# A mixture-of-experts loop in 36 tiles instead of 39: four tiles shared by two experts, split across column groups of the matmul array

## The chip, the cores and the metric

One core of a Trainium2 chip runs the whole program. The time is device microseconds of one execution, the median over several. TensorE (PE) multiplies, VectorE (DVE) and ScalarE (ACT) work element by element, GpSimd (POOL) does small arithmetic and issues the indirect DMAs, SyncE (SP) issues the plain ones. A matmul has a stationary operand (loaded first, PEld in the profile) and a moving one that streams through the array, and writes PSUM; everything else here is in SBUF or DRAM. An fp32 matmul shows as two matmul rows and two weight loads in the trace.

## The reference, cut to what matters

Eight sublayers on x of 8 x 256 tokens of 256 values. The change touches the sixth, a mixture of 8 experts, two per token:

```python
N, C = 2048, 640                         # B*T tokens, int(1.25 * N / E * K)
top_v, top_i = top_k(softmax(x_flat @ router_w.T), 2)
top_v = top_v / sum(top_v)
for k in range(2):
    eid, gate = top_i[:, k], top_v[:, k]
    pos = (place of the token among those that chose eid as their k-th) 
    keep = pos < C                        # else the token is dropped for this k
    h = gelu(einsum('ech,ehf->ecf', expert_in, w1))     # 256 -> 1024
    y = einsum('ecf,efh->ech', h, w2)                   # 1024 -> 256
    out = out + y[slot] * (gate * keep)[:, None]
x = x + tanh(g_ffn[2]) * out
```

## The kernel before

The 4096 pairs of a token and an expert are sorted by expert and cut into tiles of 128 rows, each of one expert. With 8 experts 4096 / 128 + 7 = 39 tiles (`MT`) are enough for any split, and 39 are always computed; unused rows point at spare rows. Both weight matrices of all experts lie in the SBUF tile `experts`.

**Routing** ends in one long chain on DVE (`Chain.link` is an instruction and a wait for it, `Chain.step` an instruction alone). It makes each expert's first tile (`til`, `end`, `off`) from the counts `cnt`, each pair's place (`cumo`, `where`), one-hot matrices that PE multiplies to invert the order (`spots`, `onehot`, L2578), and from them `rown` (the row to gather for each place), `eid` (the expert of each tile), `gidx` (where its gate lies) and `dest` (the row to add to). PE runs matmuls without use (`warm`) meanwhile.

**The loop** runs over tiles j. POOL gathers the 128 rows of tile j from DRAM (L731, into `xsb`, three buffers), three tiles behind it the gates (L737), and six behind it adds a finished tile to `token_sum` in DRAM by an indirect DMA with addition (L747, from `ysb`, three buffers); a scatter waits until the one before has landed, since two tiles may hold one token. DVE copies the expert's first matrix into `tilew` in two halves (`tile_weights`, L1833, each with a register load of the expert's number, L1831, ahead of it) and the turned rows into `xTb` (L1867). On PE, in the order of the program:

- `rows_t(j+1)`, L2593: two transposes of a gathered tile;
- `first(j)`, L2605: rows to the 1024 hidden values, `tilew` stationary, the 128 rows moving, so that the hidden values come out turned; 16 matmuls of 128 columns, the second half first (semaphores `m_hh`, then `m_h`);
- `second(j-1)`, L2616: eight matmuls of 256 columns, `hidT` stationary, the second expert matrix moving straight out of `experts` at an address in a register.

ACT applies gelu to the two PSUM banks of `first` (L1198) and scales the result by the gate into `ysb` (L1207). So each of these has the time of another tile's matmuls to finish.

**SP** loads the weights of the next layer (`w3a`, `w3b`, `w3f`, `bc3`, `b2`, L494 to L496) ahead of the loop, then the second half of the start values of `token_sum` (L476), and the gates (L501).

Of the kernel before, what the change touches and what calls it, by code (L numbers as in the profile page):

```python
# [13 lines left out]
B, S, D = 8, 256, 256  # L14
# [16 lines left out]
MT = B * S * 2 // P + E - 1  # L31
# [8 lines left out]
def build(nc, a, out, phases=8):  # L40
# [10 lines left out]
    with ctx:  # L51
# [143 lines left out]
        cols = sb("cols", [P, 20])  # L195
# [45 lines left out]
        dest = sb("dest", [P, MT], i32)  # L241
        gate2 = sb("gate2", [P, TT, 2])
        eid = sb("eid", [P, MT], i32)
# [9 lines left out]
        ye = post[3].rearrange("p (t d) -> p t d", t=TB)  # L253
        onehot = [w[:, 0:2, :].rearrange("p c s -> p (c s)").bitcast(bf16).rearrange("p (v n) -> p v n", n=P) for w in wk]
# [20 lines left out]
        STORES = KEPT + 2 * 16  # L275

# [79 lines left out]
        m_ys = counted("m_ys")  # L356
        s_bw2 = sem("s_bw2")
# [30 lines left out]
        GATED = 40  # L388
# [40 lines left out]
        def _(sp):  # L429
# [27 lines left out]
            if phases >= 6:  # L457
# [40 lines left out]
                sp.wait_ge(m_xp.sem, m_xp.past(2))  # L498
                base_rows(B // 2, B)
                sp.wait_ge(rt_v.sem, rt_v.past(GATED))  # L500
                sp.dma_start(gate_d.rearrange("(p n) o -> p (n o)", p=P), gsent).then_inc(s_kd, 16)  # L501
                for u in range(3):
                    sp.wait_ge(s_st[u], MT // 3 * 16)
# [14 lines left out]
        def _(gp):  # L518
# [205 lines left out]
            if phases >= 6:  # L724
# [3 lines left out]
                for j in range(MT + 6):  # L728
                    if j < MT:
                        gp.wait_ge(m_xp.sem, m_xp.past(max(j - 2, 0)))  # L730
                        gp.indirect_dma_start(xsb[j % 3], None, xs_d,  # L731
                                              bass.IndirectOffsetOnAxis(ap=rown[:, j:j + 1], axis=0)
                                              ).then_inc(s_ld[j % 3], 16)
                    if j == 3:
                        gp.wait_ge(s_kd, STORES)
                    if 0 <= j - 3 < MT:
                        gp.indirect_dma_start(gslot[:, j - 3:j - 2], None, gate_d,  # L737
                                              bass.IndirectOffsetOnAxis(ap=gidx[:, j - 3:j - 2], axis=0)
                                              ).then_inc(s_ld[j % 3], 16)
                    if j == 6:  # L740
                        gp.wait_ge(inv_d, 1)
                    if j >= 6:
                        i, u = j - 6, (j - 6) % 3
                        gp.wait_ge(m_ys.sem, m_ys.past(i + 1))
                        if i:
                            gp.wait_ge(s_st[(i - 1) % 3], 16 * ((i - 1) // 3 + 1))
                        gp.indirect_dma_start(acc_d, bass.IndirectOffsetOnAxis(ap=dest[:, i:i + 1], axis=0),  # L747
                                              ysb[u], None, compute_op=ALU.add).then_inc(s_st[u], 16)
# [31 lines left out]
        def _(ac):  # L780
# [401 lines left out]
            if phases >= 6:  # L1182
# [18 lines left out]
                def result(j):  # L1201

                    ac.wait_ge(m_y.sem, m_y.past(j + 1))
                    if j >= 3:
                        ac.wait_ge(s_st[j % 3], 16 * (j // 3))
                    ac.wait_ge(s_ld[j % 3], landed(j + 3))
                    nc.scalar.activation(ysb[j % 3], bank(4)[:, 0:D], ACT.Copy, scale=gslot[:, j:j + 1]  # L1207
# [109 lines left out]
        def _(ve):  # L1317
# [237 lines left out]
            if phases >= 4:  # L1555
# [108 lines left out]
                def l5_zeros():  # L1664
                    nc.vector.memset(sum0[:, lead - 16:lead], 0.0).then_inc(rt_n.sem, 1)
                    nc.vector.memset(small[:, 0:36], 0.0).then_inc(rt_n.sem, 1)
# [80 lines left out]
            if phases >= 5:  # L1747
# [7 lines left out]
                for b in range(B - 4, B - 1):  # L1755
# [6 lines left out]
                til, til2, til3, end = small[:, 0:12], small[:, 12:24], small[:, 24:36], small[:, 36:44]  # L1762
                off, raw = small[:, 48:64], small[:, 64:80]
# [3 lines left out]
                c5.link(nc.vector.tensor_tensor(raw[:, 0:8], cnt[:, 0:8], cnt[:, 8:16], ALU.add))  # L1767
                c5.link(nc.vector.tensor_scalar(raw[:, 8:16], raw[:, 0:8], 1.0 / P, (P - 1) / (2.0 * P),
                                                ALU.mult, ALU.add))
                c5.link(nc.vector.tensor_scalar(raw[:, 0:8], raw[:, 8:16], MAGIC, None, ALU.add))  # L1770
                c5.link(nc.vector.tensor_scalar(til[:, 4:12], raw[:, 0:8], MAGIC, None, ALU.subtract))
                c5.link(nc.vector.tensor_tensor(til2[:, 4:12], til[:, 4:12], til[:, 3:11], ALU.add))
                c5.link(nc.vector.tensor_tensor(til3[:, 4:12], til2[:, 4:12], til2[:, 2:10], ALU.add))
                c5.link(nc.vector.tensor_tensor(end, til3[:, 4:12], til3[:, 0:8], ALU.add))
                c5.link(nc.vector.tensor_tensor(raw[:, 0:8], end, til[:, 4:12], ALU.subtract))
                c5.link(nc.vector.tensor_scalar(off[:, 0:8], raw[:, 0:8], float(P), -1.0, ALU.mult, ALU.add))
# [6 lines left out]
                                                off.unsqueeze(1).broadcast_to([P, TT, 16]), ALU.add))  # L1783
                c5.link(nc.vector.tensor_tensor(hit, cumo, oh, ALU.mult))
# [22 lines left out]
                for k in range(3):  # L1807
# [11 lines left out]
                past = ptall[:, 5 * MT:5 * MT + 7 * MT].rearrange("p (n e) -> p n e", e=E - 1)  # L1819
                ef = here.rearrange("p q j -> p (q j)").bitcast(f32)[:, 0:MT]  # L1820
                c5.link(nc.vector.tensor_tensor(past, iota[:, 0:MT].unsqueeze(2).broadcast_to([P, MT, E - 1]),
                                                end[:, 0:E - 1].unsqueeze(1).broadcast_to([P, MT, E - 1]), ALU.is_ge))
# [988 lines left out]
```

## Time and profile before

| | |
|---|---|
| median of 3 runs | 961.45 us (958.54 to 962.52) |
| the profiled execution | 959.38 us, of which the span from first to last instruction is 957.6 |
| PE busy | 834.3 us, 87% |
| DVE, ACT, POOL busy | 623.9, 511.4, 546.1 us |
| loop over 39 tiles | about 557 to 843 us of the span |

A busy share is an average over stages. What bounds a stage is read there: which engine has no idle time, and what the others wait for.

### The profile page before, as it was taken

The page shows a single profiled execution, that of the slowest core. Times are in us where ns is not written, and L with a number is a line of the kernel's source. Part 1 is how long each engine was busy: PE and PEld are TensorE (multiplying, and loading weights), DVE is VectorE, ACT ScalarE, POOL GpSimd, SP SyncE. Part 2 cuts the span into 40 slices and gives each one's busy share as a digit, 9 for nine tenths or more (in the row PEclk, how much of TensorE's full clock was granted, in tenths as well). Part 3 has the DMA queues.
Part 4 walks back from the last instruction along what each step waited for, and adds up shares of the span by engine and source line. Part 5 has one row for each costly group of instructions (what it writes and reads, how often), then busy time and mean ns, then how long its engine had stood idle before and what let it go on. Part 6 is the DMA issues. An engine that isn't in the chain of part 4 may idle for free.

```text
span 957.6 us, 18599 instructions
## 1 busy us (share of the span) xinstructions
PE 834.3 (87%) x5752; PEld 677.1 (71%) x5758; DVE 623.9 (65%) x2655; ACT 511.4 (53%) x1302; POOL 546.1 (57%) x743
## 2 busy tenths in 40 slices
PE   6899999997665767768877889999999999998895
PEld 5677767885443434546666689999999999977774
DVE  3877767889988999999996733222222222516784
ACT  3777755689985778788776212212212122226762
POOL 2566445585652887888676054455455455237882
PEclk9999999998997788989999799999999999999997
DMA  9100001000000090000000932222222222130001
GB/s 292 43 1 2 2 2 44 1 2 1 1 1 1 13 383 2 2 24 24 23 29 18 359 121 40 34 40 35 39 39 35 40 34 39 18 100 1 21 25 44
DMA packets 38027, 47.20 MB, mean 49 GB/s; under 512 B 4502, under 2 KB 33918, under 8 KB 37931
## 3 DMA queue, kind: packets, MB, share of 16 engines
q1 hardware_dynamic: 29195, 35.77, 11.0%
q0 software_dynamic: 8736, 10.25, 6.8%
q8 instruction: 48, 0.79, 0.4%
q14 instruction: 48, 0.39, 0.1%
HBM read 34.46 MB, written 11.55 MB: 48 GB/s over the span
## 4 chain that ended last, share of the span: by engine, by line
PE 59%; DVE 23%; POOL 6%; issue 6%; ACT 4%; DMA 2%; SPq 0%; DVEq 0%; POOLq 0%; ACTq 0%
PE ps L2605 14%; PE ps L2616 14%; DVE experts L1596 4%; DVE experts L1586 4%; PE ps L2098 3%; PE ps L2121 3%; DVE m L1581 2%; DVE m8b L1591 2%; PE ps L2085 2%; PE ps L2108 2%; PE ps L2045 1%; DVE mx L1578 1%; DVE sm L1519 1%; PE ps L2391 1%; PE ps L2016 1%
## 5 line engine op out<-in xcount | busy, mean ns | idle before, releaser
L1833 DVE COPY ptall<-experts 128x512 f32 x156 | 59.9, 426 | 154.6 <-PE ps L2605 132.5
L2605 PE MATMUL ps<-xnT,ptall 128*128 128x128 f32 x1248 | 145.8, 275 | 0.3 <-DVE ptall L1833 0.3
L2616 PE MATMUL ps<-experts,wk 128*128 x624 | 141.8, 380 | 2.5 <-ACT xkeep L1207 1.4
L2605 PEld LDWEIGHTS ps<-xnT,ptall 128*128 128x128 f32 x1248 | 142.5, 192 | 0.5 <-issue 0.5
L2616 PEld LDWEIGHTS ps<-experts,wk 128*128 128x128 f32 x624 | 115.7, 191 | 17.4 <-issue 3.6
L1198 ACT ACTIVATE wk<-ps 128x1024 f32<-128x1024 f32 x39 | 39.9, 1024 | 158.0 <-PE ps L2605 149.0
L731 POOL DMA_INDIRECT xn<-expert_in,rown x39 | 38.7, 991 | 125.8 <-PE ps L2593 98.7
L747 POOL DMA_INDIRECT token_sum<-xkeep,dest x39 | 64.2, 1647 | 36.1 <-ACT xkeep L1207 21.9
L648 POOL TENSOR_TENSOR experts<-experts,mx 128x616 f32<-128x616 f32 x32 | 39.1, 1223 | 53.6 <-DVE experts L1596 53.4
L565 POOL TENSOR_TENSOR experts<-experts,rden 128x616 f32<-128x616 f32 x32 | 38.8, 1215 | 46.1 <-DVE rden L1376 46.1
L1075 ACT ACTIVATE experts<-experts 128x77 f32<-128x77 f32 x256 | 64.2, 259 | 0.1
L2016 PE MATMUL ps<-ones 128*128 128x256 bf16 x436 | 57.5, 291 | 5.8 <-POOL mone L523 5.8
L2016 PEld LDWEIGHTS ps<-ones 128*128 128x128 bf16 x436 | 44.7, 105 | 15.0 <-ACTq L784 5.8
L1596 DVE MATCH_REPLACE8 experts<-m8b,experts 128x80 f32<-128x80 f32 x256 | 54.4, 225 | 0.0
L1586 DVE MATCH_REPLACE8 experts<-m,experts 128x80 f32<-128x80 f32 x256 | 54.4, 225 | 0.0
L2411 PE MATMUL ps<-ident,experts 128*77 128x128 f32 x256 | 36.4, 289 | 20.0 <-POOL experts L676 18.6
L787 ACT ACTIVATE experts<-ps 128x512 f32<-128x512 f32 (+2 forms) x56 | 39.6, 712 | 26.2 <-PE ps L2045 20.5
L673 POOL TENSOR_TENSOR rden<-ssum,mone 128x8 f32<-128x8 f32 x32 | 52.5, 1642 | 1.3 <-ACT experts L1075 1.3
L1207 ACT ACTIVATE xkeep<-ps,ptall 128x256 f32<-128x256 f32 x39 | 18.5, 473 | 65.2 <-PE ps L2616 65.2
L2422 PE MATMUL ps<-ptall,experts 77*32 77x256 f32 x256 | 22.8, 431 | 34.3 <-ACT ptall L1083 29.3
L787 ACT ACTIVATE ptall<-ps 77x512 f32<-77x512 f32 (+1 forms) x80 | 41.2, 545 | 21.5 <-PE ps L2098 18.2
L2411 PEld LDWEIGHTS ps<-ident,experts 128*77 128x77 f32 x256 | 30.8, 157 | 27.6 <-issue 26.8
(326 smaller groups left out, 2135.6 us busy)
## 6 DMA issues: line engine op xcount, KB each, us to landing
experts<-in_ew SPq DMA_DIRECT2D x16, 1024.0 KB, 11.5
x<-in_x SPq DMA_DIRECT2D x1, 2048.0 KB, 10.8
xkeep<-in_bw SPq DMA_DIRECT2D x2, 1024.0 KB, 7.1
expert_in<-xkeep SPq DMA_DIRECT2D x8, 256.0 KB, 4.2
x<-token_sum SPq DMA_DIRECT2D x8, 256.0 KB, 3.2
out<-x SPq DMA_DIRECT2D x8, 256.0 KB, 2.1
token_sum<-x SPq DMA_DIRECT2D x4, 256.0 KB, 2.5
token_sum<-x SPq DMA_DIRECT2D x1, 1024.0 KB, 4.5
```

The source lines that it names most:

```text
L673: n = own_p.mark(nc.gpsimd.tensor_tensor(rden[u][:, :], ssum[u][:, :], mone[:, :], ALU.pow))
L747: gp.indirect_dma_start(acc_d, bass.IndirectOffsetOnAxis(ap=dest[:, i:i + 1], axis=0), ysb[u], None, compute_op=ALU.add).then_inc(s_st[u], 16)
L787: return nc.scalar.activation(dst, src, ACT.Copy)
L1075: ins = nc.scalar.activation(row, row, ACT.Exp, scale=-1.0, accum_out=ssum[u][:, j:j + 1])
L1198: nc.scalar.activation(hidT[j % 2].rearrange("p (v n) -> p v n", v=2), ps[j % 2][:, :, :], ACT.Gelu).then_inc(m_g.sem, 1)
L1586: ins = nc.vector.match_replace(d[j], m8[u][:, j, :], d[j], -BIG)
L1596: ins = nc.vector.match_replace(d[j], m8b[u][:, j, :], d[j], -BIG)
L1833: ins = nc.vector.tensor_copy(tilew[:, v, c, :], experts[:, bass.ds(e * EW + (c * FF + v * 512), 512)])
L2016: nc.tensor.matmul(bank(b)[:, 0:2 * P], hot[:, 0:P], hot, start=True, stop=True)
L2411: ins = nc.tensor.transpose(ps[2][0:KEYS, h // 2, at:at + P], pr[i % 2][:, t, h * KEYS:(h + 1) * KEYS], ident[:, :])
L2605: ins = nc.tensor.matmul(ps[j % 2][:, v, k * P:(k + 1) * P], tilew[:, v, c, k * P:(k + 1) * P], xTb[j % 3][:, c, :], start=c == 0, stop=c ...
L2616: ins = nc.tensor.matmul(bank(4)[:, 0:D], hidT[j % 2][:, k * P:(k + 1) * P], experts[:, bass.ds(e * EW + (E * EW + k * D), D)], start=k == ...
```

## The change

`MT` becomes 36: 32 wide tiles of one expert each, and at the places 3, 6, 9 and 12 of the loop (`MIXED_AT`) mixed tiles of two units of 64 rows, each unit with an expert of its own (`OWNERS` = 32 + 8 numbers in `eid`). Counted in units, 4096 / 64 + 7 = 71 are enough, and there are 72. Rows past the 32nd wide tile are moved to the units in the routing.

A mixed tile can't keep two weight sets stationary over 128 moving rows. `first_mixed` turns the roles: 64 rows of a unit are stationary in one half of the array's columns, and 512 hidden values move; unit 0 writes PSUM partitions 0 to 63 with weights from `experts`, unit 1 writes 64 to 127 with weights from `tilew`. The hidden values then come out by rows, so that `turn_mixed` turns them (eight transposes into `ps[3]`), DVE copies them back (`hidden_turned`), and `second_mixed` works in two column groups again, unit 1 with its second matrix out of `w2b`, which DVE fills by four copies (`unit_weights`). `w2b` lies in `xkeep[:, 0:8]`, where the next layer's weights go, so SP loads those after the last mixed tile's result. A mixed tile may hold one token twice, so its scatter is split: first unit 0's 64 rows, then, when that has landed, all 128 with unit 0's rows sent to spare rows.

```diff
-MT = B * S * 2 // P + E - 1
+UNIT = 64
+WIDE = 32
+MIXED_AT = (3, 6, 9, 12)
+MT = WIDE + MIXED
+OWNERS = WIDE + UNITS * MIXED
...
+        w2b = xkeep[:, 0:8, :].rearrange("p t d -> p (t d)")
...
+                sp.wait_ge(m_xp.sem, m_xp.past(2))
+                base_rows(B // 2, B)
+                sp.wait_ge(rt_v.sem, rt_v.past(GATED))
+                sp.dma_start(gate_d.rearrange("(p n) o -> p (n o)", p=P), gsent).then_inc(s_kd, 16)
+                sp.wait_ge(m_y.sem, m_y.past(MIXED_AT[-1] + 1))
                 for w, key in ((w3a, "w3a"), (w3b, "w3b"), (w3f, "w3f")):
                     sp.dma_start(w, a[key].rearrange("(c p) n -> p c n", p=P)).then_inc(s_w[7], 16)
...
+                        if i in MIXED_AT:
+                            gp.indirect_dma_start(acc_d, bass.IndirectOffsetOnAxis(ap=dest[0:UNIT, at:at + 1], axis=0),
+                                                  ysb[u][0:UNIT, :], None, compute_op=ALU.add).then_inc(s_st[u], 16)
+                            gp.wait_ge(s_st[u], scattered(i) - 16)
+                            gp.indirect_dma_start(acc_d, bass.IndirectOffsetOnAxis(ap=dest[:, MT + at:MT + at + 1], axis=0),
+                                                  ysb[u], None, compute_op=ALU.add).then_inc(s_st[u], 16)
...
+                past_wide, by_expert = (v.rearrange("p (q e) -> p q e", e=E) for v in (hit, cumo))
+                c5.link(nc.vector.tensor_tensor(past_wide, by_expert, edge[:, 4:12].unsqueeze(1)
+                                                .broadcast_to([P, 2 * TT, E]), ALU.is_ge))
+                c5.link(nc.vector.tensor_tensor(past_wide, past_wide, jump.unsqueeze(1)
+                                                .broadcast_to([P, 2 * TT, E]), ALU.mult))
+                c5.link(nc.vector.tensor_tensor(cumo, cumo, hit, ALU.add))
...
+                nc.vector.tensor_scalar(dest[:, MT:MT + MIXED], dest[:, 0:MIXED], cols[:, 20:21], cols[:, 21:22],
+                                        ALU.mult, ALU.add).then_inc(inv_d, 1)
...
+                def unit_weights(j):
+                    m = MIXED_AT.index(j)
+                    if m:
+                        ve.wait_ge(m_y.sem, m_y.past(MIXED_AT[m - 1] + 1))
+                    at = owner(j, UNITS - 1)
+                    e = ve.value_load(eid[0:1, at:at + 1], min_val=0, max_val=E - 1)
+                    for q in range(4):
+                        ins = nc.vector.tensor_copy(w2b[:, q * 512:(q + 1) * 512],
+                                                    experts[:, bass.ds(e * EW + (E * EW + q * 512), 512)])
+                    ins.then_inc(m_w2.sem, 1)
+
+                def hidden_turned(j):
+                    ve.wait_ge(m_tp.sem, m_tp.past(MIXED_AT.index(j) + 1))
+                    nc.vector.tensor_copy(hidT[j % 2].rearrange("p (v n) -> p v n", v=2), ps[3][:, :, :]
+                                          ).then_inc(m_tc.sem, 1)
...
                         tile_weights(j - 1, 1)
                         tile_weights(j - 1, 0)
+                    if j - 1 in MIXED_AT:
+                        unit_weights(j - 1)
+                    if j - 2 in MIXED_AT:
+                        hidden_turned(j - 2)
                     ve.wait_ge(m_xp.sem, m_xp.past(j + 1))
...
+                def first_mixed(j):
+                    pe.wait_ge(m_xs.sem, m_xs.past(j + 1))
+                    pe.wait_ge(m_g.sem, m_g.past(j - 1))
+                    e = pe.value_load(eid[0:1, owner(j):owner(j) + 1], min_val=0, max_val=E - 1)
+                    for v in (1, 0):
+                        pe.wait_ge(m_w.sem, m_w.past(2 * j + 2 - v))
+                        for c in range(CH):
+                            nc.tensor.matmul(ps[j % 2][0:UNIT, v, :], xTb[j % 3][:, c, 0:UNIT],
+                                             experts[:, bass.ds(e * EW + (c * FF + v * 512), 512)],
+                                             start=c == 0, stop=c == CH - 1)
+                            ins = nc.tensor.matmul(ps[j % 2][UNIT:P, v, :], xTb[j % 3][:, c, UNIT:P], tilew[:, v, c, :],
+                                                   start=c == 0, stop=c == CH - 1)
...
+                def second_mixed(j):
+                    m = MIXED_AT.index(j)
+                    pe.wait_ge(m_tc.sem, m_tc.past(m + 1))
+                    pe.wait_ge(m_w2.sem, m_w2.past(m + 1))
+                    pe.wait_ge(m_ys.sem, m_ys.past(j))
...
-                        first(j)
+                        (first_mixed if j in MIXED_AT else first)(j)
                     if j >= 1:
-                        second(j - 1)
+                        (second_mixed if j - 1 in MIXED_AT else second)(j - 1)
+                    if j in MIXED_AT:
+                        turn_mixed(j)
```

PE before, within one tile: `rows_t`, `first`, and the start of `second` (`ISA` rows work out an address in a register):

```order
L2593 MATMUL ps<-ident,xn 128x128 x2
L2605 MATMUL ps<-xnT,ptall 128x128 x16
L2614 TENSOR_LOAD eid
L2614 ISA x2
L2616 ISA
L2616 MATMUL ps<-experts,wk 128x256
```

PE of the change, from the end of the `second` that follows `first_mixed(3)` to `second_mixed(3)`:

```order
L2688 MATMUL ps<-experts,wk 128x256
L2714 MATMUL ps<-ident,wk 128x128 x8
L2665 MATMUL ps<-ident,xn 128x128 x2
L2677 MATMUL ps<-xnT,ptall 128x128 x16
L2723 TENSOR_LOAD eid
L2723 ISA x2
L2725 ISA
L2725 MATMUL ps<-experts,wk 64x256
L2728 MATMUL ps<-xkeep,wk 64x256
```

The eight transposes stand behind `second(2)`, and a whole `first` lies between them and the matmuls that use what they turned.

DVE before, in the routing, from the tile ends to each pair's place:

```order
L1776 TENSOR_SCALAR ptall<-ptall 128x8
L1777 TENSOR_TENSOR ptall<-ptall,xn 128x8
L1780 TENSOR_TENSOR xn<-ps,xn 128x256
L1781 TENSOR_TENSOR xn<-xn,ptall 128x256
L1784 TENSOR_TENSOR xnT<-xn,wk 128x256
```

DVE of the change, the same place:

```order
L1815 SCALAR_TENSOR_TENSOR ptall<-ptall 128x8
L1817 TENSOR_TENSOR ptall<-ptall,xn 128x8
L1820 TENSOR_TENSOR xn<-ps,xn 128x256
L1821 TENSOR_TENSOR xn<-xn,ptall 128x256
L1825 TENSOR_TENSOR xnT<-xn,ptall 128x256
L1827 TENSOR_TENSOR xnT<-xnT,ptall 128x256
L1829 TENSOR_TENSOR xn<-xn,xnT 128x256
L1830 TENSOR_TENSOR xnT<-xn,wk 128x256
```

Three instructions of 256 elements have come in between. POOL of the change, at the scatters of tiles 2 and 3:

```order
L778 DMA token_sum<-xkeep,dest 2176x256
L753 DMA xn<-expert_in,rown 128x256
L760 DMA ptall<-token_gates,ptall 128x1
L772 DMA token_sum<-xkeep,dest 2176x256
L775 DMA token_sum<-xkeep,dest 2176x256
L753 DMA xn<-expert_in,rown 128x256
```

Before, one scatter (L747) stood where L772 and L775 do, and the next gather followed it at once.

## Rows read from the trace of the kernel before

**Rows 1.** Windows of the loop: length, busy time of engines, granted clock, DMA.
```profile
core 0: us, PE busy (x) PEld busy (x) DVE busy (x) ACT busy (x) POOL busy (x), PEclk, DMA share, GB/s
...
557.00:843.00 286.00, 283.07 (x1947) 264.35 (x1948) 83.00 (x216) 59.20 (x78) 134.60 (x113) 1.00 0.23 39
```

**Rows 2.** Who waited for whom in the loop: total, times, longest.
```profile
ACT wk L1198 <- PE ps L2605: 149.0, 36, 4.4
DVE ptall L1833 <- PE ps L2605: 132.5, 66, 2.1
POOL xn L731 <- PE ps L2593: 98.7, 33, 3.8
```

**Rows 3.** Timeline of one tile: start, duration, engine, line [idle before <-releaser].
```profile
642.80 0.38 PE L2593 MATMUL ps<-ident,xn 128*128 128x128 f32 x2
...
643.02 3.74 PE L2605 MATMUL ps<-xnT,ptall 128*128 128x128 f32 x32
...
643.46 0.98 POOL L731 DMA_INDIRECT xn<-expert_in,rown  x1 [3.04 <-PE ps L2593]
...
645.75 0.76 DVE L1833 COPY ptall<-experts 128x512 f32 x2 [2.11 <-PE ps L2605]
646.01 1.66 POOL L747 DMA_INDIRECT token_sum<-xkeep,dest  x1 [0.30 <-issue]
...
646.59 3.62 PE L2616 MATMUL ps<-experts,wk 128*128 x16
647.82 1.02 ACT L1198 ACTIVATE wk<-ps 128x1024 f32<-128x1024 f32 x1 [4.34 <-PE ps L2605]
648.55 0.77 DVE L1833 COPY ptall<-experts 128x512 f32 x2 [2.04 <-PE ps L2605]
```

**Rows 4.** Timeline of PE: tiles 2 and 3, early in the loop.
```profile
572.51 1.26 PE L2616 MATMUL ps<-experts,wk 128*128 x4
574.80 2.93 PE L2616 MATMUL ps<-experts,wk 128*128 x12 [1.03 <-issue]
577.58 0.38 PE L2593 MATMUL ps<-ident,xn 128*128 128x128 f32 x2
577.79 3.74 PE L2605 MATMUL ps<-xnT,ptall 128*128 128x128 f32 x32
```

**Rows 5.** Timeline of PE: the last tile's first layer.
```profile
831.24 3.74 PE L2605 MATMUL ps<-xnT,ptall 128*128 128x128 f32 x32
```

**Rows 6.** Timeline of PE in the first attention, matmuls on parts of the array.
```profile
84.82 0.56 PE L2085 MATMUL ps<-experts,wk 64*128 64x154 f32 x6
85.22 1.03 PE L2071 MATMUL ps<-experts 64*128 64x256 f32 x8
86.18 0.64 PE L2108 MATMUL ps<-ptall,experts 77*32 77x256 f32 x8
86.74 0.66 PE L2098 MATMUL ps<-ident,experts 128*77 128x128 f32 x4
87.34 0.79 PE L2085 MATMUL ps<-experts,wk 64*128 64x154 f32 x8
88.06 0.66 PE L2098 MATMUL ps<-ident,experts 128*77 128x128 f32 x4
88.56 1.25 PE L2121 MATMUL ps<-experts,xkeep 128*128 128x256 f32 x5
```

**Rows 7.** The same for weight loads (PEld).
```profile
86.17 0.16 PEld L2108 LDWEIGHTS ps<-ptall,experts 77*32 77x32 f32 x8 [0.33 <-issue]
```

**Rows 8.** Timeline of DVE: the end of the routing and the copies before tile 0.
```profile
539.02 0.17 DVE L1777 TENSOR_TENSOR ptall<-ptall,xn 128x8 f32<-128x8 f32 x1
539.22 0.42 DVE L1780 TENSOR_TENSOR xn<-ps,xn 128x256 f32<-128x256 f32 x1
539.68 0.42 DVE L1781 TENSOR_TENSOR xn<-xn,ptall 128x256 f32<-128x256 f32 x1
...
541.70 0.19 DVE L1790 SCALAR_TENSOR_TENSOR ptall<-ptall 128x32 f32<-128x32 f32 x1
541.81 1.45 DVE L1791 TENSOR_TENSOR ptall<-iota,ptall 128x1248 bf16<-128x1248 f32 x1
543.37 1.46 DVE L1795 TENSOR_TENSOR ptall<-ptall,iota 128x1248 bf16<-128x1248 bf16 x1
...
555.90 0.76 DVE L1833 COPY ptall<-experts 128x512 f32 x2 [0.77 <-issue]
556.58 0.42 DVE L1867 COPY xnT<-ps 128x256 f32<-128x256 f32 x1
```

**Rows 9.** The scatters from 600 to 800 us.
```profile
DMA to landing us min/median/max: 3.7/3.9/4.3
```

**Rows 10.** The page's costliest groups: weight loads of the first layer.
```profile
L2605 PEld LDWEIGHTS ps<-xnT,ptall 128*128 128x128 f32 x1248 | 142.5, 192 | 0.5 <-issue 0.5
```

More of the change, by code:

```diff
@@ L30 @@
 PADDED = KEYS + 16 - DROP
-MT = B * S * 2 // P + E - 1
+UNIT = 64
+UNITS = P // UNIT
+WIDE = 32
+MIXED_AT = (3, 6, 9, 12)
+MIXED = len(MIXED_AT)
+MT = WIDE + MIXED
+OWNERS = WIDE + UNITS * MIXED
+assert B * S * 2 // UNIT + E - 1 <= UNITS * MT and UNITS * MIXED >= E
 PAIRS = B // 2
@@ L240, in build @@
         rown = sb("rown", [P, MT], i32)
-        dest = sb("dest", [P, MT], i32)
+        dest = sb("dest", [P, MT + MIXED], i32)
         gate2 = sb("gate2", [P, TT, 2])
-        eid = sb("eid", [P, MT], i32)
+        eid = sb("eid", [P, OWNERS], i32)
         xsb = [xn[0][:, 0, :], xn[0][:, 1, :], xn[1][:, 0, :]]
@@ L275, in build, with column, owner, scattered @@
         STORES = KEPT + 2 * 16
+        def column(j):
+            return MIXED_AT.index(j) if j in MIXED_AT else MIXED + j - sum(m < j for m in MIXED_AT)
+        def owner(j, unit=0):
+            return WIDE + UNITS * MIXED_AT.index(j) + unit if j in MIXED_AT else column(j) - MIXED
+        def scattered(j):
+            return 16 * sum(UNITS if i in MIXED_AT else 1 for i in range(j % 3, j + 1, 3))
         def landed(j):
@@ L387, in build @@
         TERN = 16
-        GATED = 40
+        GATED = 48
         def rows2(b):
@@ L1204, in result @@
                     if j >= 3:
-                        ac.wait_ge(s_st[j % 3], 16 * (j // 3))
+                        ac.wait_ge(s_st[j % 3], scattered(j - 3))
                     ac.wait_ge(s_ld[j % 3], landed(j + 3))
-                    nc.scalar.activation(ysb[j % 3], bank(4)[:, 0:D], ACT.Copy, scale=gslot[:, j:j + 1]
+                    at = column(j)
+                    nc.scalar.activation(ysb[j % 3], bank(4)[:, 0:D], ACT.Copy, scale=gslot[:, at:at + 1]
                                          ).then_inc(m_ys.sem, 1)
@@ L1760, in _ @@
                 ve.wait_ge(rt_n.sem, rt_n.past(TT + 4))
-                til, til2, til3, end = small[:, 0:12], small[:, 12:24], small[:, 24:36], small[:, 36:44]
-                off, raw = small[:, 48:64], small[:, 64:80]
+                til, til2, til3, ends = (small[:, 24 * k:24 * k + 24].rearrange("p (g n) -> p g n", g=2) for k in range(4))
+                off, raw, edge = small[:, 256:272], small[:, 272:288], small[:, 288:300]
                 where, tl, rr, pos = (small[:, 96 + 32 * k:128 + 32 * k] for k in range(4))
@@ new lines, in turn_mixed @@
+                def turn_mixed(j):
+                    m = MIXED_AT.index(j)
+                    pe.wait_ge(m_g.sem, m_g.past(j + 1))
+                    if m:
+                        pe.wait_ge(m_tc.sem, m_tc.past(m))
+                    for k in range(FF // P):
+                        ins = nc.tensor.transpose(ps[3][:, k // 4, k % 4 * P:(k % 4 + 1) * P],
+                                                  hidT[j % 2][:, k * P:(k + 1) * P], ident[:, :])
+                    ins.then_inc(m_tp.sem, 1)
@@ new lines, in second_mixed @@
+                def second_mixed(j):
+                    m = MIXED_AT.index(j)
+                    pe.wait_ge(m_tc.sem, m_tc.past(m + 1))
+                    pe.wait_ge(m_w2.sem, m_w2.past(m + 1))
+                    pe.wait_ge(m_ys.sem, m_ys.past(j))
+                    e = pe.value_load(eid[0:1, owner(j):owner(j) + 1], min_val=0, max_val=E - 1)
+                    for k in range(FF // P):
+                        nc.tensor.matmul(bank(4)[0:UNIT, 0:D], hidT[j % 2][:, k * P:k * P + UNIT],
+                                         experts[:, bass.ds(e * EW + (E * EW + k * D), D)], start=k == 0,
+                                         stop=k == FF // P - 1)
+                        ins = nc.tensor.matmul(bank(4)[UNIT:P, 0:D], hidT[j % 2][:, k * P + UNIT:(k + 1) * P],
+                                               w2b[:, k * D:(k + 1) * D], start=k == 0, stop=k == FF // P - 1)
```

78 lines of the change are left out of this document (48 added, 30 removed).

## Prediction

> **What bounds the kernel now.** I read the loop's windows first. Over 286 us PE is busy for 283, at a granted clock of 1.00, which is 2.4 GHz; DVE, ACT and POOL are busy for 83, 59 and 135 [rows 1]. Then the waits: the three longest sums in the loop are all waits for PE [rows 2]. So in this stage each us of PE's matmuls is a us of the program, and the other engines matter only where they make PE wait. The timeline of one tile shows how far they are from that [rows 3]: rows turned at 642.80, the first layer from 643.02, the second from 646.59, without a gap. From tile 3 (577.79 us) to tile 38 (831.24) there are 35 periods [rows 4, 5], 253.45 / 35 = 7.24 us each. What lies ahead of the loop is DVE's chain: it ends with the copies at 555.90 and 556.58, and tile 0 starts behind them [rows 8].
>
> **Three tiles less.** 3 x 7.24 = 21.7 us of PE, all on the path: -21.7.
>
> **Four mixed tiles, each against a plain one.** I count in rounds, a round being the matmuls that stream at the same time.
>
> *First layer.* A plain `first` is 32 pieces of 128 columns: 3.74 - 0.27 (the last one's own latency) over 31 gives 0.112 each, 3.58 us in all [rows 3]. `first_mixed` is 8 matmuls of 512 columns, 16 pieces. If both column groups stream together they are 8 rounds. 256 columns take (3.62 - 0.38) / 15 = 0.216 [rows 3], so 512 take 0.43, and 8 rounds 3.44: -0.14.
>
> Do they stream together? The trace has no two groups of 64 columns under full rows. Its neighbours lie on both sides of it. L2108 has four groups of 32 columns on 77 rows: eight pieces of 256 columns end in 0.64 us, two rounds; one after the other they would need 8 x 0.216 = 1.7. L2071 has two groups of 64 rows: eight pieces in 1.03, four rounds of (1.03 - 0.38) / 3 = 0.218 [rows 6]. I take two at a time at the full pace, since L2108 divides the array by columns, as the change does, and even streams four. Between L2108's rounds lie 0.26 at most (0.64 - 0.38); that is the upper bound of a round of 256 columns, 0.04 more than I take.
>
> *Switching.* A change of the array's division costs something. Where nothing changes, a group starts 0.16 before the one ahead has ended (88.06 + 0.66 against 88.56). L2108 starts only 0.07 before (85.22 + 1.03 against 86.18), and its two rounds take 0.64 where 0.60 is due: 0.13 for entering. L2098 behind it starts 0.08 before the end, and needs 0.66 for 0.60: 0.14 for leaving. Entering L2085, by row groups, costs 0.20: it starts 0.06 before the end, and its four rounds take 0.79, where three take 0.56 at 84.82 and the fourth adds 0.13 [rows 6]. A mixed tile enters and leaves twice: 0.54 to 0.68, I take 0.64, near the middle, as 64 columns are nearer to 32 by kind and to 128 by the load.
>
> *The turn.* Eight transposes; two take 0.38 with 0.27 latency, so 0.11 each [rows 3]: 0.88. All on PE's path.
>
> *Second layer.* 16 matmuls of 256 columns, 32 pieces, 16 rounds x 0.216 = 3.46, as much as the plain one: 0. By the bound of 0.26 a round it would be +0.7, and the first layer +0.3 by the same addition per round.
>
> Together -0.14 + 0.64 + 0.88 = 1.38 a tile, 5.5 for four (bounds 5.1 and 9.8).
>
> **Ahead of the loop.** DVE's chain sets the end there, so all of it counts. The small part was 10 waited instructions of 0.20 (one at 539.02, the next at 539.22 [rows 8]) and is now 11 waited and 3 unwaited ones, an unwaited one costing 0.11 (541.70 to 541.81): +0.2 + 0.33 = 0.5. The three new ones of 256 elements cost as much as L1780, 0.46 from start to start: +1.4. L1791 and L1795 shrink by 3 in 39 of 1.45 each: -0.2. The comparison that makes `eid` is two instructions for one, and `dest` gets one more, before the copy of tile 0's second half: about 0.1 and 0.2, by the small rows. Sum +2.0. PE's warming matmuls and the weight loads are no cover, since PE waits for this chain.
>
> **What is moved at no cost, and what hides it.**
> - The register load ahead of `first_mixed` (PE had one only ahead of `second`): the queue of PE holds the matmuls of the tile before, as it does for `second`, which starts without a gap behind `first` [rows 3].
> - `turn_mixed` waits for gelu. Gelu starts at 647.82, 1.06 after the modelled end of `first` at 646.76, and takes 1.02 [rows 3]; so the hidden values are there some 2.1 us after the first layer, and `second(j-1)` covers 3.46. Behind the waiting transposes are queued the rows' transposes and `first(j+1)`; 1.3 us of cover are left.
> - DVE's copy of the turned values: 1024 elements out of PSUM. 256 take 0.42 [rows 8]; at that rate per element 1.7 is the upper end, ACT's gelu over the same shape with 1.02 the lower; I take 1.2. It is covered by `first(j+1)`, 3.6. Behind it on DVE stand the rows' copy, wanted a tile later, and the tile weights of j+2.
> - `unit_weights`: four copies and a register load. A pair of copies takes 0.76, and the halves' copies end at 649.32, 0.9 ahead of the next `first` at 650.27 (643.02 + 7.24) [rows 3]. So DVE is done 1.3 us behind that start; the rows' copy it delays is wanted 7 us behind it, and the next weights' copy can only start about then anyway.
> - The split scatter. POOL issues the scatter at 646.01, and the next gather is due at 643.46 + 7.24 = 650.7. The first half lands 3.9 us after its issue [rows 9], the second is issued for 1.66, so POOL is free at about 651.8, 1.1 late, and the next scatter waits for the landing at some 654.1 in place of 653.25. Gathers run three tiles ahead and `ysb` has three buffers: no cost. Its cover is gone only if POOL is late by two tiles.
> - SP's five loads go behind tile 12's result. 1.4 MB then meet gathers and scatters with tiles to spare; the loads are wanted 190 us later. What SP does behind them (L508) comes after the loop. Ahead of the loop the DMA engines get less to do, but DVE is the later one there: no gain.
> - The early stall at 573.77 to 574.80 (1.03, in `second(1)`) [rows 4] lies ahead of the first mixed tile. I leave it; without it 1 to 1.5 us would go too.
>
> **The sum.** -21.7 + 5.5 + 2.0 = -14.2. Against the profiled execution, 959.38 (span 957.6), that is 945.2. This execution was 2.1 below the median of 961.45, within the spread of the three; against the median it is 947.2. I take the middle, **946.2**.
>
> **The rivals.**
>
> *Column groups take turns.* Then first and second layer of a mixed tile cost 3.44 and 3.46 more, 27.6 for four tiles: 946.2 + 27.6 = 973.8, slower. It decides from 14.2 / 4 = 3.6 us a tile on, which is when a round costs half as much again. Against it: L2108 [rows 6]. For it: 64 columns and 128 moving rows in each of two streams stand in no row. Chance 0.04.
>
> *Loads aren't hidden in this mode.* Each of the 24 rounds then begins with its weight load. Eight loads of 32 columns take 0.16 together, and the single load behind a round would be 0.1 to 0.19 (0.19 for the 128 columns of L2605 [rows 10]): 2.4 to 4.6 a tile, 10 to 18 in all, 956 to 964. Against it: L2108's eight loads, for both of its rounds, are all done at 86.33, while the first round streams [rows 7]. Chance 0.07. "TensorE: Matmul & The Clock Gate" of the Trainium skill (The mechanism, in Part 3) says that a load overlaps matmuls in flight only when its row group is another one, and elsewhere that the background buffer allows it too. By its first sentence this rival would hold, as both units use all rows; L2108's loads share their rows and overlap, so the trace speaks for the second.
>
> *The middle comes late.* One of the covers above is thinner than read (gelu to transposes 1.3 us, DVE's load in a mixed tile), and PE waits 1 to 2 us in each mixed tile: 950 to 954. For it: `tilew`, the unit's weights, the turned values and the rows' copies stand on one queue, and each wait holds back all behind it. Chance 0.13.
>
> **How the numbers follow.** Forecast 0.76 (942 to 950), the middle late 0.13, loads 0.07, turns 0.04. The measurement can tell about 0.5% from no change, that is 956.6. Faster: 0.76 + 0.13 = 0.89, less a little for the unknown, 0.88. Same: most of the loads' rival, 0.07. Slower: 0.05. The range 941 to 955 takes in the forecast with the bounds of its switching and rounds (the upper, 9.8 for 5.5, gives 950.5) and the late middle.
>
> **What would show it.** In the profile after: 32 plain periods of 7.24; the PE rows of `first_mixed` as x16 over some 3.6 us and those of `second_mixed` x32 over 3.8, transposes x8 over 1.05; a mixed tile 1.4 longer than a plain one, and no idle time on PE ahead of the transposes or of `second_mixed`; the loop starting 2 us later, and as long from its end to the program's as before. PE rows of 6.9 us would show turns, rounds of 0.35 the loads, idle time with DVE or ACT as releaser the late middle. The prediction is wrong if a mixed tile costs over 3 us more than a plain one, or if the chain ahead of the loop grows by more than 3.

## The result, and the profile after

The changed kernel takes 946.5 us (median of 4 runs, 946.26 to 947.93), the kernel before on the same chip 960.0 (957.81 to 962.52). The ratio is 0.9861, with a 95% interval of 0.9838 to 0.9885. The forecast was 946.2 with a range of 941 to 955. On a second chip the same two kernels took 941.5 and 956.3, a ratio of 0.9845 (0.9826 to 0.9864).

So the change saves 1.4%, and both intervals lie clear of no change. The agreement hides a term that was missed, and short stalls that some of the profiled executions have and others don't. To see them, the profiled span is cut at three instructions that both kernels have: the difference of the two gates (L1758 before, L1790 after), the first matmul of tile 0, and the small matmul behind the loop (L2633, L2746).

| part of the profiled span, us | before | after | difference | forecast |
|---|---|---|---|---|
| start to the gates' difference | 536.57 | 539.05 | +2.48 | 0 |
| to tile 0 | 20.82 | 23.81 | +2.99 | +2.0 |
| the loop | 286.00 | 269.17 | -16.83 | -16.2 |
| behind the loop | 114.2 | 114.1 | -0.1 | 0 |
| span | 957.6 | 946.1 | -11.5 | -14.2 |

The marks before and after:

```profile
536.57 0.17 DVE L1758 TENSOR_TENSOR gate<-topv 128x16 f32<-128x16 f32 x1
557.39 3.74 PE L2605 MATMUL ps<-xnT,ptall 128*128 128x128 f32 x32
843.39 0.95 PE L2633 MATMUL ps<-cols,xkeep 128*128 128x1 f32 x8
```

```profile
539.05 0.17 DVE L1790 TENSOR_TENSOR gate<-topv 128x16 f32<-128x16 f32 x1
562.86 3.74 PE L2677 MATMUL ps<-xnT,ptall 128*128 128x128 f32 x32
832.03 0.95 PE L2746 MATMUL ps<-cols,xkeep 128*128 128x1 f32 x8
```

The first part holds no instruction that the change touches, apart from a memset of 96 for 36 elements. In the ten profiles taken later the gates' difference came between 535.3 and 539.3 us, and the last part took 111.3 to 114.2 us, in no order that follows their edits. So a difference of some 3 us between two profiled spans says little, and terms are read inside a stage.

The loop's windows of the kernel after (columns as in rows 1):

```profile
core 0: us, PE busy (x) PEld busy (x) DVE busy (x) ACT busy (x) POOL busy (x), PEclk, DMA share, GB/s
563.00:832.00 269.00, 266.64 (x1829) 234.26 (x1828) 88.61 (x219) 54.68 (x72) 130.96 (x107) 1.00 0.26 45
```

PE is still the bound: 266.6 of 269 us at the full clock. DVE is busier than before in a shorter loop (88.6 in 269 against 83.0 in 286 [rows 1]), by the units' weights and the copies back.

A mixed tile (number 6) on PE, with the rows of unit 1's matmuls left out, which start 0.01 us behind unit 0's:

```profile
605.57 0.38 PE L2665 MATMUL ps<-ident,xn 128*128 128x128 f32 x2
605.88 0.64 PE L2700 MATMUL ps<-experts,xnT 128*64 x1
606.36 0.59 PE L2700 MATMUL ps<-experts,xnT 128*64 x1
...
608.94 0.59 PE L2700 MATMUL ps<-experts,xnT 128*64 x1
609.47 3.72 PE L2688 MATMUL ps<-experts,wk 128*128 x16
613.02 1.04 PE L2714 MATMUL ps<-ident,wk 128*128 128x128 f32 x8
613.90 0.38 PE L2665 MATMUL ps<-ident,xn 128*128 128x128 f32 x2
614.12 3.74 PE L2677 MATMUL ps<-xnT,ptall 128*128 128x128 f32 x32
617.78 0.43 PE L2725 MATMUL ps<-experts,wk 128*64 x1
618.05 0.38 PE L2725 MATMUL ps<-experts,wk 128*64 x1
```

Rounds of 512 columns are 0.43 apart and rounds of 256 columns 0.215, as if the other group weren't there. No row of this tile has an idle time in brackets: neither the transposes nor `second_mixed` waited. The first mixed tile, number 3, is another matter in this one profile:

```profile
577.95 2.97 PE L2688 MATMUL ps<-experts,wk 128*128 x13
581.07 0.91 PE L2688 MATMUL ps<-experts,wk 128*128 x3 [0.15 <-issue]
...
582.76 0.64 PE L2700 MATMUL ps<-experts,xnT 128*64 x1 [0.56 <-DVE ptall L1883]
```

`second(1)` takes 3.87 us to the next rows (581.82) in place of 3.46, and PE waits 0.56 us for DVE's copy into `tilew`: 1.0 in all. The changed kernel's second profile shows neither.

The other engines in the stretch of tile 6:

```profile
604.97 1.62 DVE L1894 COPY xkeep<-experts 128x512 f32 x4
606.50 0.41 DVE L1939 COPY xnT<-ps 128x256 f32<-128x256 f32 x1
...
614.10 1.22 DVE L1900 COPY wk<-ps 128x1024 f32<-128x1024 f32 x1 [2.87 <-PE ps L2714]
```

```profile
609.58 1.03 ACT L1229 ACTIVATE wk<-ps 128x1024 f32<-128x1024 f32 x1 [3.34 <-PE ps L2703]
```

The copy back is done at 615.32, and `second_mixed` starts at 617.78, so that 2.5 us of cover are left. Gelu is done at 610.61, 2.4 ahead of the transposes.

Ahead of the loop, the small part of DVE's chain and the three new instructions (L1825 to L1829), to be compared with rows 8:

```profile
541.78 0.16 DVE L1815 SCALAR_TENSOR_TENSOR ptall<-ptall 128x8 f32<-128x8 f32 x1
...
542.18 0.42 DVE L1820 TENSOR_TENSOR xn<-ps,xn 128x256 f32<-128x256 f32 x1
...
543.09 0.43 DVE L1825 TENSOR_TENSOR xnT<-xn,ptall 128x256 f32<-128x256 f32 x1
543.55 0.43 DVE L1827 TENSOR_TENSOR xnT<-xnT,ptall 128x256 f32<-128x256 f32 x1
544.01 0.42 DVE L1829 TENSOR_TENSOR xn<-xn,xnT 128x256 f32<-128x256 f32 x1
544.47 0.42 DVE L1830 TENSOR_TENSOR xnT<-xn,wk 128x256 f32<-128x256 f32 x1
```

Before, the product is L1784:

```profile
540.14 0.42 DVE L1784 TENSOR_TENSOR xnT<-xn,wk 128x256 f32<-128x256 f32 x1
```

They cost what was forecast: from the gates' difference to L1820 3.13 us where it was 2.65 to L1780 (+0.48), and from there to the product L1830 2.29 where it was 0.92 (+1.37). What wasn't forecast stands on PE behind it, where the one-hot matrices are multiplied (L2650, L2578 before; L2088 and L2016 are the useless matmuls of `warm`):

```profile
550.24 0.42 PE L2650 MATMUL ps<-ptall,wk 128*128 128x72 bf16 x8 [2.40 <-DVE wk L1848]
...
551.88 1.48 PE L2088 MATMUL ps<-ones 128*128 128x256 bf16 x6
```

And the same place before:

```profile
546.11 0.46 PE L2578 MATMUL ps<-ptall,wk 128*128 128x78 bf16 x8 [1.13 <-DVE wk L1802]
546.40 0.82 PE L2016 MATMUL ps<-ones 128*128 128x256 bf16 x6
```

PE now stands idle for 2.40 us in place of 1.13 ahead of the first product, and the granted clock is at its half level, 1.2 GHz, from 551 to 554 us, so that six useless matmuls take 1.48 in place of 0.82.

### The profile page after: what moved, and what is told of

It reads as the page before. It is cut to its first block, busy times and chain, and to the rows that moved or that the text cites. A ratio compares the mean times of both kernels' runs of the same rounds, so it can differ in the third digit from the quotient of the medians.

```text
span 946.1 us, 18344 instructions
## 1 busy us (share of the span) xinstructions
PE 819.8 (87%) x5634; PEld 649.5 (69%) x5640; DVE 631.3 (67%) x2669; ACT 507.1 (54%) x1296; POOL 544.5 (58%) x738
## 4 chain that ended last, share of the span: by engine, by line
PE 56%; DVE 27%; issue 5%; POOL 5%; ACT 4%; DMA 1%; another core or an unknown queue 1%; SPq 0%; DVEq 0%; POOLq 0%; ACTq 0%
PE ps L2677 12%; PE ps L2688 11%; DVE experts L1618 5%; DVE experts L1628 5%; PE ps L2170 3%; DVE m L1613 3%; DVE m8b L1623 3%; PE ps L2193 3%; PE ps L2088 3%; PE ps L2157 2%; DVE mx L1610 2%; PE ps L2180 2%; DVE sm L1551 2%; PE ps L2117 2%; PE ps L2700 1%
## 5 line engine op out<-in xcount | busy, mean ns | idle before, releaser
L1883 DVE COPY ptall<-experts 128x512 f32 x144 | 56.7, 434 | 129.1 <-PE ps L2677 109.1
L2677 PE MATMUL ps<-xnT,ptall 128*128 128x128 f32 x1024 | 119.6, 275 | 0.2 <-DVE ptall L1883 0.2
L2688 PE MATMUL ps<-experts,wk 128*128 x512 | 116.6, 380 | 1.6 <-ACT xkeep L1239 1.4
L2677 PEld LDWEIGHTS ps<-xnT,ptall 128*128 128x128 f32 x1024 | 116.9, 192 | 0.5 <-issue 0.4
L1229 ACT ACTIVATE wk<-ps 128x1024 f32<-128x1024 f32 x36 | 36.9, 1025 | 145.8 <-PE ps L2677 125.6
L2688 PEld LDWEIGHTS ps<-experts,wk 128*128 128x128 f32 x512 | 94.7, 190 | 17.1 <-issue 5.6
L753 POOL DMA_INDIRECT xn<-expert_in,rown x36 | 36.2, 1006 | 107.4 <-PE ps L2665 69.5
L778 POOL DMA_INDIRECT token_sum<-xkeep,dest x32 | 52.6, 1643 | 34.0 <-ACT xkeep L1239 25.6
L2088 PE MATMUL ps<-ones 128*128 128x256 bf16 x436 | 59.4, 296 | 5.8 <-POOL mone L544 5.8
L2088 PEld LDWEIGHTS ps<-ones 128*128 128x128 bf16 x436 | 45.4, 106 | 15.4 <-ACTq L815 5.8
## 6 DMA issues: line engine op xcount, KB each, us to landing
x<-in_x SPq DMA_DIRECT2D x1, 2048.0 KB, 11.5
```

The source lines that it names most:

```text
L1883: ins = nc.vector.tensor_copy(tilew[:, v, c, :], experts[:, bass.ds(e * EW + (c * FF + v * 512), 512)])
L2088: nc.tensor.matmul(bank(b)[:, 0:2 * P], hot[:, 0:P], hot, start=True, stop=True)
L2677: ins = nc.tensor.matmul(ps[j % 2][:, v, k * P:(k + 1) * P], tilew[:, v, c, k * P:(k + 1) * P], xTb[j % 3][:, c, :], start=c == 0, stop=c ...
L2688: ins = nc.tensor.matmul(bank(4)[:, 0:D], hidT[j % 2][:, k * P:(k + 1) * P], experts[:, bass.ds(e * EW + (E * EW + k * D), D)], start=k == ...
```

## Experiments

Each kernel's loop and the stretch ahead of it, measured between the instructions named above. Three of the loops hold an early stall: 1.6 us in the kernel before, 1.0 in the first profile of the kernel after, 0.8 in the one with blocks of four. The median of a kernel is to be compared only with that of the kernel before in its group, beside it in brackets.

| kernel | median, us | ahead of the loop | loop |
|---|---|---|---|
| before, profiled once | 960.0 | 20.82 | 286.00 |
| after, profiled first | 946.5 (960.0) | 23.81 | 269.17 |
| after, again | 941.5 (956.3) | 23.96 | 268.17 |
| before with 36 tiles | 935.7 (957.6) | 20.53 | 262.67 |
| after, mixed tiles computed plainly | 939.5 (957.6) | 23.96 | 262.68 |
| after, groups apart | 953.8 (957.6) | 23.96 | 278.88 |
| after, groups in blocks of four | 949.3, one run (957.3) | 23.94 | 273.06 |
| after, one scatter | 942.7 (956.3) | 23.92 | 268.16 |
| after, 80 useless matmuls | 942.2 (957.6), 943.5 (956.3) | 22.54, 22.54 | 268.18, 268.19 |
| the same, product made four times | 946.0 (956.3) | 25.19 | 268.13 |
| the same, mixed tiles at 12, 17, 22, 27 | 944.9 (957.3) | 22.53 | 268.18 |

**1. Three tiles less, alone.**

```diff
-MT = B * S * 2 // P + E - 1
+MT = 36
```

> The kernel before with 36 plain tiles and nothing else of the change; pairs that would fall into tiles 37 to 39 are left out. My account: three periods of 7.24 us go and nothing else, 960.0 - 21.7 = 938.3. Rival (something besides PE's matmuls, the DMAs or the start of the loop, sets part of the loop's length): less than 20 us.

Measured: 935.7 us (ratio 0.9785, 0.9751 to 0.9818), 21.9 below the kernel before in its group. The first and last marks of its loop:

```profile
558.81 3.74 PE L2605 MATMUL ps<-xnT,ptall 128*128 128x128 f32 x32
...
821.48 0.95 PE L2633 MATMUL ps<-cols,xkeep 128*128 128x1 f32 x8
```

The loop is 23.33 shorter than in the profile of before. Three periods make 21.7 of that, and the other 1.6 is the early stall [rows 4], which isn't there in this run. The interval of the medians, 17.4 to 23.8 us, would leave room for the rival's "less than 20"; the loop doesn't.

**2. What a mixed tile adds.**

```diff
-                        (first_mixed if j in MIXED_AT else first)(j)
+                        first(j)
                     if j >= 1:
-                        (second_mixed if j - 1 in MIXED_AT else second)(j - 1)
-                    if j in MIXED_AT:
-                        turn_mixed(j)
+                        second(j - 1)
...
-                    if j - 1 in MIXED_AT:
-                        unit_weights(j - 1)
-                    if j - 2 in MIXED_AT:
-                        hidden_turned(j - 2)
```

> The changed kernel with its four mixed tiles computed as plain ones on TensorE and VectorE (no turned roles, no transposes, no second weights, no copy back); the second unit's expert is left out, its rows get the first unit's weights. Routing, split scatter and late loads stay. My account: a mixed tile costs 1.38 us more than a plain one (0.34 of switching in each layer, 0.88 of transposes, 0.14 less in the first layer's stream), so 5.5 us go: 941.0. Rival (the mixed tiles also cost through VectorE or GpSimd): more than 7 us go.

Measured: 939.5 us (ratio 0.9823, 0.9791 to 0.9855), and in the trace a loop from 560.40 to 823.08, 262.68, where experiment 1 has 262.67:

```profile
560.40 3.74 PE L2673 MATMUL ps<-xnT,ptall 128*128 128x128 f32 x32
...
823.08 0.95 PE L2740 MATMUL ps<-cols,xkeep 128*128 128x1 f32 x8
```

Against the 268.17 of the changed kernel's second profile (562.42 to 830.59) four mixed tiles cost 5.49, or 1.37 each; 1.38 was forecast. That the loop equals experiment 1's also shows that the routing's other numbers, the late loads and the split scatter, all still in this kernel, cost the loop nothing.

**3. Do neighbours have to be of different groups?**

```diff
                         for c in range(CH):
                             nc.tensor.matmul(ps[j % 2][0:UNIT, v, :], xTb[j % 3][:, c, 0:UNIT],
...
+                        for c in range(CH):
                             ins = nc.tensor.matmul(ps[j % 2][UNIT:P, v, :], xTb[j % 3][:, c, UNIT:P], tilew[:, v, c, :],
```

and the same in `second_mixed`, eight matmuls of unit 0 and then eight of unit 1.

> The changed kernel with the matmuls of a mixed tile in another order: all of unit 0's and then all of unit 1's, in each half of the first layer and in the second. If column groups stream together only where neighbours in program order use different groups, the first layer needs 13 rounds of 0.43 in place of 8 and the second 31 of 0.216 in place of 16: 5.4 us a tile, 21.6 in all, 968. Rival (the queue starts the other group's matmuls ahead of their turn): no change, 946.5.

Measured: 953.8 us (ratio 0.9963, 0.9947 to 0.9979), loop 278.88, 10.7 more than in the changed kernel's second profile: half of one expectation, and neither is right as it stands. The first layer paid next to nothing (3.63 us to the next matmuls in place of 3.59), though four pieces of unit 0 stand ahead of four of unit 1 in the program (a piece is one of the two matmul rows that an fp32 matmul makes). The second shows what the queue does (L2726 is unit 0, L2730 unit 1):

```profile
592.84 3.02 PE L2726 MATMUL ps<-experts,wk 128*64 x13
595.48 0.43 PE L2730 MATMUL ps<-xkeep,wk 128*64 128x256 f32 x1
595.69 0.38 PE L2726 MATMUL ps<-experts,wk 128*64 x1
...
595.91 0.38 PE L2726 MATMUL ps<-experts,wk 128*64 x1
...
596.12 0.38 PE L2726 MATMUL ps<-experts,wk 128*64 x1
596.18 2.97 PE L2730 MATMUL ps<-xkeep,wk 128*64 128x256 f32 x13
```

Unit 1's first piece starts at 595.48, ahead of three pieces of unit 0 that stand before it in the program. So matmuls of another column group start out of program order, here ahead of three waiting pieces and no more. In the first layer's blocks of four that is enough to pair them. Twelve pieces of unit 0 and twelve of unit 1 stream alone: 12 x 0.216 = 2.6 a tile is the price, and 4 x 2.6 = 10.4 of the 10.7. Four rounds still pair, so streaming together is worth at least these 2.6 us in the second layer.

**4. How far ahead?** `second_mixed` with four matmuls (eight pieces) of unit 0, four of unit 1, and again:

```diff
+                    for k0 in (0, 4):
+                        for k in range(k0, k0 + 4):
...
+                        for k in range(k0, k0 + 4):
```

> The changed kernel with second_mixed in blocks: four matmuls of unit 0, four of unit 1, four of 0, four of 1 (eight pieces each). From the run with the groups apart, where a second group's pieces began about four pieces ahead of their turn: if the queue looks about four pieces ahead, a block of eight hides half, 24 to 25 rounds of 0.216 in place of 16, 1.9 us a tile, and the loop takes 276 us. Rival (the queue looks far enough ahead for eight): 268.3. Rival (strict order): 30 rounds, 280.

Measured, in a single run: loop 273.06, 4.9 more than with alternating units. Of that 0.8 is an early stall like that of the changed kernel's first profile (PE idle for 0.29 and 0.25 us at tiles 2 and 3). The rest is the second layers: in each of the four mixed tiles `second_mixed` takes 4.63 us to the next matmuls in place of 3.61, so the price is 1.0 a tile. Without the stall the loop is 272.3, and none of the three expectations (276, 268.3, 280) is right. The rows of unit 1 in tile 3, the first and the last:

```profile
593.12 0.43 PE L2730 MATMUL ps<-xkeep,wk 128*64 128x256 f32 x1
...
595.66 1.24 PE L2730 MATMUL ps<-xkeep,wk 128*64 128x256 f32 x5
```

Unit 0 starts at 592.20, and unit 1's first piece behind five of its first eight, so again ahead of three. From there on the two groups stay paired, through the change of blocks too, and the head start is paid once and not in each block as I had counted: unit 1 starts 0.92 us late here, and 2.64 late in experiment 3 (592.84 to 595.48), where the price was 2.6.

**5. The useless matmuls.**

```diff
-                warm(60, 3)
+                warm(80, 3)
```

> The changed kernel with 80 in place of 60 useless matmuls while VectorE's routing chain runs. In the profile after, the longer chain leaves TensorE idle for longer ahead of the inversion, and the granted clock is half from 550.9 to 554.3 us, where it was full before; from the first one-hot matrix to the copy out of the inversion it then takes 6.28 us against 5.07. If the longer chain outran the useless matmuls, this takes back 1.2 us ahead of the loop (945.3), with the clock at 1.0 there. Rival (the half clock there is a chance of that one execution): no change.

> 80 useless matmuls once more, for a tighter interval: 22.5 us from the gate's difference to tile 0 and 1.4 us less than the changed kernel. Rival (what the clock gives there is taken back later): the median of the changed kernel.

> The changed kernel once more, as the mate of the next ones on the same chip. The early stall of its first profile (the loop took 269.3 us, against 268.3 with the same loop code and 80 useless matmuls) is a chance of the execution by my account, and the half clock ahead of the inversion is not: 24.0 us from the gate's difference to tile 0, as in the two other kernels with 60 useless matmuls and the longer chain.

Measured: ahead of the loop 22.54 in both profiles with 80, and 23.96 in the changed kernel's second one (and in experiments 2 and 3), so 1.42 goes. The second of the two with 80:

```profile
550.44 0.42 PE L2650 MATMUL ps<-ptall,wk 128*128 128x72 bf16 x8 [1.53 <-DVE wk L1848]
550.69 0.82 PE L2088 MATMUL ps<-ones 128*128 128x256 bf16 x6
```

So the half clock is no chance: all six profiles with the longer chain and 60 useless matmuls have it at this place (23.81 to 23.96 ahead of the loop), and neither of these two has it. In the stage, the cause is shown. In the whole it isn't seen. The medians with 80 are 942.2 (ratio 0.9857, 0.9820 to 0.9895) and 943.5 (0.9857, 0.9831 to 0.9883), the changed kernel's beside the latter 941.5 (0.9845, 0.9826 to 0.9864). The parts ahead of the gates and behind the loop differ by up to 4.0 and 2.9 us from profile to profile. Whether some of the gain is taken back there, or it drowns, stays open.

**6. Is DVE's chain the path?**

```diff
+                for _ in range(4):
-                c5.link(nc.vector.tensor_tensor(hit, cumo, oh, ALU.mult))
+                    c5.link(nc.vector.tensor_tensor(hit, cumo, oh, ALU.mult))
```

on top of the 80 useless matmuls (and the count of the chain's steps, `GATED`, raised by three).

> 80 useless matmuls, and in the routing chain the product of 256 elements made four times in place of once, with the same values. My account: VectorE's chain sets the start of the loop, so the three come out at full price, 3 x 0.46 = 1.4 us more than with 80 alone: 23.9 us from the gate's difference to tile 0. Rival (part of the chain's growth is covered, by the gather of the first tile or the weights): less than 0.7.

Measured: 25.19 ahead of the loop, 2.65 more than with 80 alone; 1.4 was expected. The four products take 1.80 where one takes 0.42, so 1.38 is the three at full price. The other 1.3 is the clock again, with PE's rows of the inversion taking 4.8 us in place of 3.5:

```profile
543.58 1.80 DVE L1831 TENSOR_TENSOR xnT<-xn,wk 128x256 f32<-128x256 f32 x4
```

```profile
550.72 0.64 PE L2651 MATMUL ps<-ptall,wk 128*128 128x72 bf16 x8 [2.90 <-DVE wk L1849]
551.16 1.47 PE L2089 MATMUL ps<-ones 128*128 128x256 bf16 x6
```

With the chain longer, 80 don't suffice either. In these profiles PE was idle there for 1.13 and 1.53 us with the clock staying full, and for 2.40, 2.90 and (the changed kernel's second) 3.70 with the clock falling to half for about 3.4 us. How long the useless matmuls last is itself set by the clock: the first 60 took 9.48 us in the changed kernel's first profile, where it rose to full at about 544.0, and 8.18 in the second, where it rose at about 540.8.

**7. One scatter for a mixed tile.**

```diff
-                        if i in MIXED_AT:
-                            gp.indirect_dma_start(acc_d, bass.IndirectOffsetOnAxis(ap=dest[0:UNIT, at:at + 1], axis=0),
...
+                        if True:
```

and the counts that others wait for, in `scattered`, made to fit.

> The changed kernel with one scatter for a mixed tile in place of two; where a mixed tile holds one token twice, one of the two additions is left out. My account: GpSimd has three tiles of slack, no change. Rival (the split scatter holds something up): up to 5 us a mixed tile less, 20 in all.

Measured: 942.7 us (ratio 0.9862, 0.9833 to 0.9891) and a loop of 268.16: nothing. The split scatter makes GpSimd wait (10.0 us over four tiles in the profile after, for the first half to land) and nobody else.

**8. The mixed tiles' places.**

```diff
-MIXED_AT = (3, 6, 9, 12)
+MIXED_AT = (12, 17, 22, 27)
```

with the 80 useless matmuls.

> 80 useless matmuls, and the mixed tiles at the places 12, 17, 22 and 27 in place of 3, 6, 9 and 12. My account: a mixed tile costs 1.37 us wherever it stands, so the loop takes 268.3 us again and the time is that with 80 useless matmuls (943.5 on that chip). Rival (mixed tiles so close to each other or to the start hold each other up through VectorE or GpSimd): up to 2 us less.

Measured: 944.9 us (ratio 0.9866, 0.9832 to 0.9901), loop 268.18. The places cost nothing, and the later start of the next layer's loads doesn't either. Since all 80-matmul kernels agree with the changed kernel within their intervals, none of them is called better.

## Why the prediction came out

- **Three tiles, -21.7.** Right. In experiment 1's loop it is 21.7 without the stall, and 21.9 in the median.
- **Rounds.** Right, and the term that mattered: two groups of 64 columns under full rows stream at the pace of one. The neighbours in rows 6 (four groups of 32, two groups of 64 rows) bracketed it well. The rivals "column groups take turns" and "loads aren't hidden" both fell with the first rows after.
- **Switching and turn.** 1.38 a mixed tile was forecast, 1.37 is measured (experiment 2). From tile 6's rows the terms are: first layer entered with 0.09 of late start and a first round of 0.48 for 0.43, left with 0.10 of late start and 0.10 in the matmuls behind it, 0.34 in all; transposes 0.88 (613.02 to 613.90); in the second layer 0.09 and 0.05, and 0.09 and 0.06, 0.29 in all; and the first layer's stream 0.14 less, as forecast.
- **The chain, +2.0.** Wrong by 1.0 in the first profile and 1.1 in the second. Its instructions were sized right: small part +0.48 for 0.5, three products +1.37 for 1.4. The prediction had named a growth of over 3 as a sign of being wrong, and 2.99 and 3.14 lie on both sides of that line. The step that failed is the sentence that the warming matmuls are no cover, which left the clock of PE's matmuls behind the chain out of the sum. They hide nothing, but they hold the clock, and 60 of them were enough for the old chain only (experiments 5 and 6). With 80 the stretch grows by 1.72 (20.82 to 22.54) in place of 3.14, so the missed term is 1.42, and the rest was sized 0.3 too high: behind the last one-hot product, where +0.3 was forecast for `eid` and `dest`, the stretch to tile 0 grew by 0.1.
- **The early stall.** I left it in the sum and said that 1 to 1.5 us would go without it. It went: the stretch from second(1) to the next rows took 5.07 in the profile of before (572.51 to 577.58 [rows 4]), and 3.46 where nothing stalls. The changed kernel's first profile lost 1.0 around tile 3, the one with blocks of four 0.8 at the same place, and the other nine nothing. So it comes in some executions, of the kernel before and of the changed one. It holds up other engines too: gelu of tile 2 starts 3.1 us late in both of the first two profiles. Its cause wasn't tried. It would have belonged in the profile's distance from the median.
- **The covers.** Those named at no cost held: transposes, copy back, unit weights, scatter, moved loads. The rival "the middle comes late" has nothing to rest on in the changed kernel's second profile, where PE waits in no mixed tile; in the first, and in that with blocks of four, one mixed tile of four waited for `tilew`, 0.56 and 0.25 us, behind the early stall.
- **The sum.** Without the stalls the parts are +3.1 ahead of the loop and 284.4 to 268.17 in it, -16.2, so -13.1 together where -14.2 was forecast. The medians differ by 13.5 on the first chip and 14.8 on the second; their intervals (11.0 to 15.6 and 13.0 to 16.6) hold both figures, so they can't tell the missed term. That 946.2 came within 0.3 of 946.5 is in part luck: it was the middle between two bases, and the median before came out at 960.0, 1.45 below the 961.45 that one of them started from, which makes up for the missed 1.1.

## What to carry to other kernels

Count a partly filled array in rounds, and find the nearest division in the same trace for its pace and for the cost of entering and leaving it: here the sum held to 0.1 us a tile. Useless matmuls that keep the clock up are sized for the work beside them: whoever lengthens that work must count them again, and read the granted clock of the stretch after. Before a stall in a single profile goes into a sum, or is left in it, ask whether another execution has it.

## What the hardware showed beyond that

Two things that no step had counted on. The matmul queue lets a matmul of another column group start ahead of program order, though not far: with blocks of sixteen pieces and with blocks of eight, three pieces of unit 0 started behind unit 1's first (experiments 3 and 4).

And a signal from PE seems to arrive late while GpSimd is issuing a scatter. In the profile of before, gelu starts 1.0 to 1.1 us behind the modelled end of `first` in 31 of the 32 tiles in which the scatter's issue lies over that end (rows 3: end 646.76, scatter 646.01 to 647.67, gelu 647.82), and one tile shows 0.28. In the last four tiles, where the scatter is over by then, it is 0.03 to 0.04. In the changed kernel, tile 6 has the scatter only from 609.89, and gelu starts at 609.58, 0.05 behind the end at 609.53:

```profile
609.89 1.61 POOL L778 DMA_INDIRECT token_sum<-xkeep,dest  x1 [0.40 <-issue]
```

while in tile 7 (first layer 614.12 to 617.86) it lies over the end, and gelu starts at 618.88, 1.0 late:

```profile
617.11 1.66 POOL L778 DMA_INDIRECT token_sum<-xkeep,dest  x1 [0.30 <-issue]
618.88 1.03 ACT L1229 ACTIVATE wk<-ps 128x1024 f32<-128x1024 f32 x1 [5.18 <-PE ps L2677]
```

The two go together in nearly every tile; tile 3 of this profile is an exception (scatter from 585.17 to 586.78, gelu at 586.46, 0.04 behind the end). No kernel was run to set it apart, so it is an observation and not a cause. Here it costs nothing, since gelu has cover.
